# Reordering the LN2 chain and the next group's K block at each group boundary of a fused attention-read, LayerNorm and SwiGLU kernel

## The reference

```python
K     = einsum('bth,kh->btk', x, W_K)
reads = einsum('btd,hd->bth', gelu(einsum('btk,dk->btd', K, W1)), W2)
x = layernorm(x + reads)                     # LN1
gate = einsum('bsd,hd->bsh', x, w_gate / 127)
up   = einsum('bsd,hd->bsh', x, w_up / 127)
h    = silu(gate) * up
x = layernorm(x + einsum('bsh,dh->bsd', h, w_down / 127))   # LN2
```

## Time and profile before

| | |
|---|---|
| median of 3 runs | 1720.16 us (1719.47 to 1787.83) |
| profiled execution, its own time | 1719.37 us |
| its span, slowest core | 1717.8 us |
| spans of all cores | 1712.1 to 1717.8 us |
| TensorE (PE) busy | 1295.0 us, 75% |
| VectorE (DVE) busy | 573.4 us, 33% |
| ScalarE (ACT) busy | 323.0 us, 19% |
| GpSimd (POOL) busy | 98.1 us, 6% |
| mean granted TensorE clock, all cores | 0.857 to 0.861 of full speed |

### The profile page before, as it was taken

How to read it: one execution, slowest core, us unless ns; L and a number is a source line. 1 busy time by engine, 2 the same in 40 slices (tenths; PEclk the granted TensorE clock), 3 DMA queues, 4 the chain that set the end, 5 groups by cost and what they waited for, 6 DMA issues and landing times.

```text
span 1717.8 us, 24544 instructions; the slowest of 8 cores (1712.1 to 1717.8 us)
## 1 busy us (share of the span) xinstructions
PE 1295.0 (75%) x9152; PEld 938.5 (55%) x9152; DVE 573.4 (33%) x1408; ACT 323.0 (19%) x705; POOL 98.1 (6%) x189
## 2 busy tenths in 40 slices
PE   2314959697895969789595968959596896959586
PEld 1203737465573746567473746647374664737464
DVE  0201343433333343333434343343434334343433
ACT  0100121212112121211212121121212122121211
POOL 9100000000000000000000000000000000000000
PEclk9656969898896989889797988969798897979888
DMA  9996020110102011110202011020201101010000
GB/s 151 177 167 101 1 62 2 49 13 29 34 1 62 1 49 14 35 27 1 62 1 58 5 38 25 1 62 2 59 4 40 23 2 49 1 50 1 25 1 25
DMA packets 36052, 64.82 MB, mean 38 GB/s; under 512 B 5024, under 2 KB 21536, under 8 KB 35936
## 3 DMA queue, kind: packets, MB, share of 16 engines
q0 software_dynamic: 26576, 29.63, 12.0%
q1 hardware_dynamic: 9360, 33.62, 5.9%
HBM read 76.09 MB, written 16.78 MB: 54 GB/s over the span
## 4 chain that ended last, share of the span: by engine, by line
PE 71%; DVE 11%; ACT 7%; another core or an unknown queue 4%; issue 4%; DMA 1%; POOL 1%; DVEq 0%; ACTq 0%; POOLq 0%
PE pa L401 19%; PE pA L422 11%; PE pA L441 11%; PE pB L422 10%; PE pB L441 10%; PE pA L212 7%; DVE x1T L376 3%; PE pB L365 2%; DVE r L326 2%; ACT dmp L333 2%; ACT dmp L249 2%; DVE x L258 2%; ACT L135 1%; DVE r L242 1%
## 5 line engine op out<-in xcount | busy, mean ns | idle before, releaser
L401 PE MATMUL pa<-WDT,hbf 128*128 128x512 bf16 x1536 | 395.5, 380 | 31.7 <-DMA WDT<-wdT 31.4
L212 PE MATMUL pA<-xTb,WKT 128*128 128x256 bf16 x1024 | 171.0, 346 | 223.4 <-DVE r L326 130.9
L212 PEld LDWEIGHTS pA<-xTb,WKT 128*128 128x128 bf16 x1024 | 121.8, 122 | 277.9 <-issue 240.2
L441 PE MATMUL pA<-x1T,WUT 128*128 128x256 bf16 x1536 | 212.4, 284 | 36.3 <-DMA WUT<-wuT 36.3
L422 PE MATMUL pA<-x1T,WGT 128*128 128x256 bf16 x1536 | 213.2, 285 | 25.6 <-DVE x1T L376 15.7
L401 PEld LDWEIGHTS pa<-WDT,hbf 128*128 128x128 bf16 x1536 | 149.2, 98 | 139.2 <-issue 40.4
L462 DVE TENSOR_TENSOR gsb<-pA,sgb 128x256 bf16<-128x256 f32 x192 | 81.5, 425 | 397.9 <-ACT sgb L457 397.9
L422 PEld LDWEIGHTS pA<-x1T,WGT 128*128 128x128 bf16 x1536 | 154.6, 101 | 91.6 <-issue 31.9
L422 PE MATMUL pB<-x1T,WGT 128*128 128x256 bf16 x1536 | 203.3, 276 | 0.0
L441 PE MATMUL pB<-x1T,WUT 128*128 128x256 bf16 x1536 | 200.6, 274 | 0.0
L441 PEld LDWEIGHTS pA<-x1T,WUT 128*128 128x128 bf16 x1536 | 156.8, 102 | 61.2 <-issue 36.7
(11 more groups left out here) (41 smaller groups left out, 503.7 us busy)
## 6 DMA issues: line engine op xcount, KB each, us to landing
xf<-x SPq DMA_DIRECT2D x32, 512.0 KB, 3.9
out<-x SPq DMA_DIRECT2D x32, 512.0 KB, 2.7
xTb<-xT POOLq DMA_DIRECT2D x128, 64.0 KB, 2.5
WGT<-wgT POOLq DMA_DIRECT2D x8, 768.0 KB, 37.6
WUT<-wuT POOLq DMA_DIRECT2D x8, 768.0 KB, 72.1
WDT<-wdT POOLq DMA_DIRECT2D x24, 256.0 KB, 98.5
WKT<-wkT POOLq DMA_DIRECT2D x8, 256.0 KB, 13.8
W1T<-w1T POOLq DMA_DIRECT2D x8, 16.0 KB, 15.4
```

Source lines behind the costliest of these rows:

```text
L212: ins = pe.matmul(bank, WKT[:, hc * D + kc * 128: hc * D + kc * 128 + 128], xb[:, hc * GROUP:(hc + 1) * GROUP], start=(hc == 0), stop=(hc ...
L401: ins = pe.matmul(pa[t][:, sl * 512:(sl + 1) * 512], hbf[:, par * GROUP + t * 128: par * GROUP + t * 128 + 128], WDT[:, hb * D + sl * 512: ...
L441: ins = pe.matmul(pu[par], WUT[:, dc * HID + hb * 128: dc * HID + hb * 128 + 128], x1T[:, dc * GROUP:(dc + 1) * GROUP], start=(dc == 0), s ...
```

## The change

`emit_K` is split: it keeps the matmuls, and the copies go to `emit_kev(gk, parity)`. `emit_LN2` is split in four parts, and the parts are woven into LN1 of the next group. The sum and the normalisation of LN2 now work in place in `x1`, not through `r1`. Waits are now named and looked up when the lists are written out, so that a matmul may name a copy that is added later. The down matmuls of block 0 get two more waits (`sq1(g,1)` and `sq2(g-1,1)`).

The order of VectorE's list at a boundary is now: both LN2 sums, `r1stt(g,0)`, statistics of LN2 tile 0, of LN1 tile 0, of LN2 tile 1, the odd copies of `K(g+1)`, `nrm2(g-1,0)`, `nrm1(g,0)`, `r1stt(g,1)`, statistics of LN1 tile 1, `nrm2(g-1,1)`, `nrm1(g,1)`, the `xev` copies. ScalarE's is: `aT`, `sq2(g-1,0)`, `sq1(g,0)`, `sq2(g-1,1)`, three square roots, the even copies of `K(g+1)`, `sq1(g,1)`, its square root. TensorE's order stays as it was. The core of the diff:

```diff
@@ emit_K: the copies move out
+        def emit_kev(gk, parity):
+            for kc in range(parity, NDC, 2):
                 src = pkslc[kc % 2]
                 dst = kTs.ap()[:, kc * GROUP:(kc + 1) * GROUP]
@@ LN2, in place
+            def r2stt(dv, t=t, c0=c0):
+                return dv.scalar_tensor_tensor(
+                    x1[:, t * D:(t + 1) * D], pa[t][:, :], INV127_3,
+                    x1[:, t * D:(t + 1) * D],
+                    ALU.mult, ALU.add,
+                    accum_out=st_[:, c0:c0 + 1])
@@ group loop, after ao
-            if g > 0:
-                emit_LN2(g - 1)
...
+            if g + 1 < ngroups:
+                emit_K(g + 1)
+
+            if g > 0:
+                emit_ln2s(g - 1, 0)
+                emit_ln2s(g - 1, 1)
+                emit_sq2(g - 1, 0)
@@ in the loop over t of LN1, ahead of nrm1
+                if t == 0:
+                    p.add("dv", r1stt, waits=waits, event=f"r1_{g}_{t}")
+                    p.add("sc", sq1, waits=[f"r1_{g}_{t}", last_sq[0]],
+                          event=f"sq1_{g}_{t}")
+                    last_sq[0] = f"sq1_{g}_{t}"
+                    if g > 0:
+                        emit_sq2(g - 1, 1)
+                        st2a = emit_ln2_stats(g - 1, 0)
+                    ln1_info[t] = ln_stats(g, t, 0, f"r1_{g}_{t}", f"sq1_{g}_{t}")
+                    if g > 0:
+                        st2b = emit_ln2_stats(g - 1, 1)
+                    if g + 1 < ngroups:
+                        emit_kev(g + 1, 1)
+                        emit_kev(g + 1, 0)
+                    if g > 0:
+                        emit_ln2_nrm(g - 1, 0, *st2a)
+                else:
+                    p.add("dv", r1stt, waits=waits, event=f"r1_{g}_{t}")
+                    p.add("sc", sq1, waits=[f"r1_{g}_{t}", last_sq[0]],
+                          event=f"sq1_{g}_{t}")
+                    last_sq[0] = f"sq1_{g}_{t}"
+                    ln1_info[t] = ln_stats(g, t, 0, f"r1_{g}_{t}", f"sq1_{g}_{t}")
+                    if g > 0:
+                        emit_ln2_nrm(g - 1, 1, *st2b)
@@ after LN1
-            if g + 1 < ngroups:
-                emit_K(g + 1)
@@ after the last group
-        emit_LN2(ngroups - 1)
+        gl = ngroups - 1
+        emit_ln2s(gl, 0)
+        emit_ln2s(gl, 1)
+        emit_sq2(gl, 0)
+        emit_sq2(gl, 1)
+        sA = emit_ln2_stats(gl, 0)
+        sB = emit_ln2_stats(gl, 1)
+        emit_ln2_nrm(gl, 0, *sA)
+        emit_ln2_nrm(gl, 1, *sB)
```

More of the change, by code:

```diff
@@ L40, in add @@
             sem = {"pe": "pe", "dv": "dv", "sc": "sc"}.get(eng)
[L41 to L45, removed]
+        w = [name for name in waits if name is not None]
         self.ops[eng].append((fn, w, sem, n))
@@ L228, in emit_K @@
                           waits=ewaits, event=f"kev{gk}_{kc}")
[L230 to L267, removed]
@@ L270, in build_core, with emit_ln2s @@
-        emit_K(0)
+        emit_K(0)
+        emit_kev(0, 0)
+        emit_kev(0, 1)
+        last_sq = [None]
+        def emit_ln2s(gq, t):
+            c0 = stcol(gq, t, 1, 0)
+            w = [f"dn_{gq}_{NHB - 1}", f"nrm1_{gq}_{t}"]
+            def r2stt(dv, t=t, c0=c0):
[4 more added lines that the diff above has]
+                    accum_out=st_[:, c0:c0 + 1])
+            p.add("dv", r2stt, waits=w, event=f"ln2s{gq}_{t}")
@@ new lines, in emit_sq2, with sq2, emit_ln2_stats @@
+        def emit_sq2(gq, t):
+            c0 = stcol(gq, t, 1, 0)
+            def sq2(sc, t=t, c0=c0):
+                return sc.activation(dmp[:], x1[:, t * D:(t + 1) * D], AF.Square,
+                                     accum_out=st_[:, c0 + 1:c0 + 2])
+            p.add("sc", sq2, waits=[f"ln2s{gq}_{t}", last_sq[0]],
+                  event=f"sq2_{gq}_{t}")
+            last_sq[0] = f"sq2_{gq}_{t}"
+        def emit_ln2_stats(gq, t):
+            return ln_stats(gq, t, 1, f"ln2s{gq}_{t}", f"sq2_{gq}_{t}")
@@ new lines, in emit_ln2_nrm, with nrm2 @@
+        def emit_ln2_nrm(gq, t, rstd_ev, m_col, rs_col):
+            T = 2 * gq + t
+            def nrm2(dv, t=t, m_col=m_col, rs_col=rs_col):
+                return dv.tensor_scalar(
+                    x1[:, t * D:(t + 1) * D], x1[:, t * D:(t + 1) * D],
+                    st_[:, m_col:m_col + 1], st_[:, rs_col:rs_col + 1],
+                    ALU.subtract, ALU.mult)
+            p.add("dv", nrm2, waits=[rstd_ev, f"mL1_{gq}_{t}", f"sq2_{gq}_{t}"],
+                  event=f"nrm2_{gq}_{t}")
+            p.add("sy", lambda sy, t=t, T=T: sy.dma_start(
+                out=out_d[T * 128:(T + 1) * 128, :], in_=x1[:, t * D:(t + 1) * D]),
+                waits=[f"nrm2_{gq}_{t}"], sem=("soa" if T % 2 == 0 else "sob"),
+                n=16, event=f"out{T}")
@@ L314, in build_core @@
                 p.add("pe", aomm, waits=waits, event=f"ao{g}_{t}")
+            if g + 1 < ngroups:
[4 more added lines that the diff above has]
+                emit_sq2(g - 1, 0)
+            ln1_info = {}
             for t in range(NT):
@@ L322, in build_core @@
                 elif g > 0:
-                    waits += [f"sq2_{g - 1}_1", f"nrm2_{g - 1}_1"]
+                    waits += [f"sq1_{g - 1}_1", f"nrm1_{g - 1}_1"]
                 def r1stt(dv, t=t, T=T, c0=c0):
@@ L329, in r1stt, with sq1 @@
                         accum_out=st_[:, c0:c0 + 1])
-                p.add("dv", r1stt, waits=waits, event=f"r1_{g}_{t}")
-                def sq1(sc, c0=c0):
+                def sq1(sc, t=t, c0=c0):
                     return sc.activation(dmp[:], r1[:], AF.Square,
                                          accum_out=st_[:, c0 + 1:c0 + 2])
-                p.add("sc", sq1, waits=[f"r1_{g}_{t}"], event=f"sq1_{g}_{t}")
-                rstd_ev, m_col, rs_col = ln_stats(g, t, 0, f"r1_{g}_{t}", f"sq1_{g}_{t}")
+                if t == 0:
[22 more added lines that the diff above has]
+                        emit_ln2_nrm(g - 1, 1, *st2b)
+                rstd_ev, m_col, rs_col = ln1_info[t]
                 nw = [rstd_ev, f"mL0_{g}_{t}", f"r1_{g}_{t}"]
@@ L393, in emit_down @@
                 dw = [f"t2_{g}_{hb}", f"w_wd{NHB - 1}"]
-                if hb == 0 and g > 0:
-                    dw.append(f"ln2s{g - 1}_{NT - 1}")
+                if hb == 0:
+                    dw.append(f"sq1_{g}_1")
+                    if g > 0:
+                        dw += [f"ln2s{g - 1}_{NT - 1}", f"sq2_{g - 1}_{NT - 1}"]
                 def dnf(pe, hb=hb, par=par):
@@ L479, in build_core @@
             emit_down(NHB - 1)
-        emit_LN2(ngroups - 1)
-        p.ops["sy"].append((None, [("soa", p.cnt["soa"]), ("sob", p.cnt["sob"])],
-                            None, 0))
+        gl = ngroups - 1
[7 more added lines that the diff above has]
+        emit_ln2_nrm(gl, 1, *sB)
+        p.ev["_all_soa"] = ("soa", p.cnt["soa"])
+        p.ev["_all_sob"] = ("sob", p.cnt["sob"])
+        p.ops["sy"].append((None, ["_all_soa", "_all_sob"], None, 0))
         with nc.Block() as block:
@@ L513, in _run @@
         merged = {}
-        for (sname, val) in waits:
+        for name in waits:
+            sname, val = p.ev[name]
             if val > merged.get(sname, 0):
```

## The result

The changed kernel takes 1756.2 us (median of 9 runs, 1752.8 to 1763.7), the one before 1719.5 us (median of 10). The ratio is 1.022, 95% interval 1.020 to 1.023: 2.2% slower, where 0.7% was forecast (1733 us). The profiled execution has a span of 1753.0 us against 1717.8, 35.2 us more.

What follows compares the result with a forecast made beforehand. TensorE sets the end; T is the start of a group's first LN2 sum, the gate its first gate matmul. 16.1 us over 14 fronts, +0.5 (group 15), -3.1 (final LN2): +13.5 on 1719.4, 1733 us; range 1710 to 1768.

Steps and rivals of the forecast that it cites:

- The mechanism: Front of each group: K begins at T+4.88, resumes at T+9.38, but output waits on VectorE leave the gate 1.15 us later.
- The final LN2's 3.1 us: After the last group: square, square root and both `nrm2` finish sooner, 3.1 us less in all.
- Group 0: First group: a gate ready a microsecond or two later is covered by the 36.3 us wait for WUT; counted as nothing.
- group 15: Last front, without K: its last `nrm1` starts at T+21.0 where it stood at T+20.48, a loss of 0.5 us.
- How long the 48 matmuls take: Second part of K on TensorE: 5.5 us, with bounds 5.43 and 6.85, so K ends at T+14.88.
- rival B: The 48 K matmuls start cold and take 6.85 us: +1.35 us a group, +19, 1752 us; chance 0.18.
- the two landings: Output DMAs between `nrm2` and `nrm1`, twice per group: landing 2.7 us, 3.69 us from start to start without collision.
- A term that I put at nothing: From the first gate matmul to the next T: all matmuls, touched by none of the changes, so no cost.
- The step of 4.76 us: VectorE, from `nrm1(g,0)` to `nrm2(g-1,1)`: 4.76 us, taken from 928.16 to 932.92 in the old trace.
- The collision: First output DMA meets the eight xT loads after K's end: 0.6 us more, bounds 0 and +4.0.
- Rival C: First output DMA gets through only after the xT burst: +3.5 us a group, +49, 1782 us; chance 0.13.
- Rival E: Earlier K carries through because the output waits don't show: 104 us less, 1629 us; chance 0.02.

Runs made afterwards that it cites:

- e1: Changed kernel with a second `x1` buffer by group parity, so `nrm1` no longer waits for the output DMA: 1649 us, ratio 0.959 to the kernel before.
- e2: Changed kernel with both `nrm2`, and so their output DMAs, ahead of the odd K copies on VectorE, `x1` single: 1649 us, ratio 0.959 to the kernel before.
- e3: Changed kernel with copy 0 of the next K right behind `sq1(g,0)` on ScalarE: 1737 us, ratio 1.011 to the kernel before.
- e4: Changed kernel with only the xT loads moved, to wait for the seventh up block: 1826 us median including low-clock executions, ratio 1.019 to the kernel before.
- e6: e2 with e3's edit (copy 0 early on ScalarE), `x1` single: 1672 us, ratio 0.973 to the kernel before.
- e5: Changed kernel with only the copies of the next K moved back behind `nrm1(g,1)` on both engines: 1752 us, ratio 1.020 to the kernel before.
- e8: Changed kernel with xT loads waiting as in e4 and the loads of x waiting for the last `xev`: 1749 us, ratio 1.019 to the kernel before.
- e9: e6 with copy 1 of the next K moved ahead of both `nrm2` on VectorE: 1617 us, ratio 0.942 to the kernel before.
- e10: e7 with only the places of the K copies moved, each to where its block is just ready: 1518 us, ratio 0.883 to the kernel before.
- e7: Changed kernel with second `x1`, copy 0 early, LN1 between K copies, LN2's statistics and `nrm2` moved to and behind the `xev` copies: 1555 us, ratio 0.906 to before.

## Why the prediction was right or wrong

**The mechanism was right.** K starts at T+4.9 and goes on at T+9.4 to within 0.05 us; its gain of some 11 us at the copies' end does not reach the gate, because `nrm2`, output DMA and `nrm1` follow each other on VectorE. e1 and e2 show that by taking the waits away in two ways: 6% each. The final LN2's 3.1 us hold as well. Group 0 came 1.3 us sooner where nothing was counted, and group 15 lost nothing where 0.5 was.

**The step that failed is "How long the 48 matmuls take".** I took 5.5 us, by group 0, and they took 7.50, more than my upper bound of 6.85. This is rival B, which I had at 0.18 and whose 1752 us is near the result; the sign that I had named for it, a second K part near 7 us, is there. The reason I gave was that the second part would begin 4.5 us after K's begin, when the kernel before had the high clock. The windows of the changed kernel (columns as in the earlier trace rows) show that it did not have it:

```profile
940.00:942.00 2.00, 1.99 (x10) 1.04 (x8) 0.96 (x7) 1.98 (x3) 0.00 (x0) 0.50 0.00 0
...
944.00:946.00 2.00, 2.00 (x11) 1.40 (x10) 0.00 (x0) 0.37 (x1) 0.00 (x0) 0.50 0.00 0
...
948.00:950.00 2.00, 2.00 (x21) 1.76 (x19) 0.42 (x1) 0.62 (x2) 0.00 (x0) 1.00 0.04 8
```

TensorE was at 1.2 GHz all through the first part of K and still at 944 to 946, 6 to 7 us after K's begin. An equal stretch after K's begin was no ground for an equal clock. One front of this core, group 2, did have it: its last copy came at T+14.9, within 0.1 us of the forecast. Why the clock rose early in 28 of the 112 fronts and late in the rest is open; e3 shows only that it does so early every time when the gap is closed.

e3 also shows that this term was the miss. There K ends about where the forecast had it (last copy at T+14.8 on the slowest core), the waits are still in place, the gate comes at T+35.9 for T+35.8, and the kernel is 1.1% slower than before (0.7 to 1.6%) for the forecast 0.7%.

The sum with 7.5 in that term is 16.1 + 14 x 2.0 + 0.5 - 3.1 = +41.5 us; 35.2 were measured. The larger of the other terms, over 14 fronts: -7 us from the step that follows, -2.8 us since I read one gate (T+34.66) where the mean is T+34.86, +5.6 us from the two landings (4.45 and 3.93 us in this front for 4.29 and 3.69), and -1.8 us from groups 0 and 15.

**A term that I put at nothing isn't nothing on every core.** "From there to the next T all is matmuls, and the change touches none of them" holds on the slowest core: 64.87 us from the gate to the next T, 64.93 before. Core 4 had the fast K in 11 fronts, and these still took 102.05 us from T to T, where 99.68 in the kernel before and the forecast's loss of 1.15 make 100.8. The waits grew there, to 4.8 and 4.3 us, and the stretch from the gate on took 65.7 us, for 64.8 on core 4 of the kernel before.

**The step of 4.76 us was mis-read.** It is the time from `nrm1` to the next `nrm1` of the kernel before, whose last wait is a square root. The `nrm2(g-1,1)` in its place has had its square root for long and needs none of it: 4.26 us. Group 15's 0.5 us went the same way.

**The collision was about right** for the first output DMA on the slowest core: 0.6 us forecast, 0.8 measured (4.4 us with xT loads beside it, 3.6 in the fronts of groups 13 and 14, which have none, and in e4). On core 4 it was 1.2, in group 2 2.0. I had given the second landing no neighbour. It has one, the loads of x issued behind it, and lost 0.3 us by it here. Rival C, the output behind the whole burst, did not come. (Its landing should have read 8.5 us, 7.2 and 1.3, not 8.2; nothing hangs on it.) The turn-taking by packets that the Trainium skill states in "DMA: Bandwidth & Descriptors", "Queues, rings and completion order", from which the estimate was again 0.6 us, is near the 0.8 us of the slowest core and too small for core 4's 1.2. By the fit in its section "Anatomy of one DMA", which is given for software-issued DMAs, no landing of this size would be under 3.2 us; these outputs are hardware-issued, the shortest of the 32 landed in 2.6 us, and that number decides.

**Rival E is what e2 is**: the earlier K carries through once the DMA issue stands ahead of K's copies. I set it aside since the list's order forbade it. As an argument about the change that was right. The gain is smaller than E's 104 us off the forecast's 1733: the last copy came at T+17.2 there too, as in the changed kernel.

## What to carry to other kernels

When work is moved forward in an in-order queue, ask what it is moved ahead of: here an output DMA whose landing had been hidden in 8.6 us of other work came to stand between two instructions of the critical chain, twice per group. Issue a store as soon as its data is final, before anything that waits for another engine, or give the next writer another buffer. A closed gap reopens at the next queue: e6 was slower than e2 until one more copy was moved, so after each reorder look for the longest idle of the bounding engine and what stands ahead of its releaser. Read more than the slowest core before a size is given to a cause: in e4, e5 and e8 the other cores show another size.

## What the runs showed of the hardware

In the changed kernel K's first 16 matmuls took 3.3 to 3.6 us, a gap of 0.9 to 1.2 us followed, and the 48 behind it took 7.5 us in 13 of the 14 fronts of the slowest core and 5.4 to 5.7 us in 11 of the 14 of core 4. Without the gap (e3, e9, e10) 64 matmuls took 9.7 to 10.0 us where nothing else stopped them. The same program had K's 48 matmuls at 5.7 and 7.6 us in neighbouring fronts of one core (e8), so a price read from one front can be off by 2 us. Bound such a term by both levels of the clock.

A gate that comes earlier does not always end the group earlier. In the changed kernel the means over groups 3 to 14 of core 4 and core 1 are T+36.6 and T+37.7 for the gate, and 102.2 and 102.4 us from T to T: 1.1 us earlier at the gate, 0.2 us shorter. The first hidden blocks at the low clock took the rest. The second gate block (bank pB) of group 8, core 4 and then core 1:

```profile
972.05 1.91 PE L451 MATMUL pB<-x1T,WGT 128*128 128x256 bf16 x8
```

```profile
974.59 1.04 PE L451 MATMUL pB<-x1T,WGT 128*128 128x256 bf16 x8
```

What decides it is open; no run here isolates it.

The landing of a 512 KB output DMA was 2.6 us alone and up to 5.9 us with other transfers beside it (e7, which issues both outputs together and two loads of x behind them).
